# Fourth edge stage of a graph network: keys and values from 64-row matmuls on the two halves of the array

## The reference

```
q = (h @ Wq).reshape(n, 8, 16)                       # per node
wk = relu(edge_attr_64 @ k_w1 + k_b1) @ k_w2 + k_b2  # per edge, wv alike
k = sum_s sh[:, s] * (h[dst] @ Cqk[:, s, :]) * wk    # s = 0..8, 64 -> 128 columns
v = sum_s sh[:, s] * (h[dst] @ Cv[:, s, :]) * wv
attn = sum over 16 of q[src] * k                     # 8 heads
alpha = softmax of attn over the edges of a segment
x = x + batchnorm(h @ W_self + segment_sum(v * alpha) @ W_out)
```

## Time and profile before

| | |
|---|---|
| device time, three runs | 4099.88 us median, 4085.95 to 4110.83 |
| profiled execution, first to last instruction | 3379.4 us |
| fourth edge stage, first transposes to last product | 2145.3 to 3274.7 us |
| its steady part, 2260 to 3250 us | PE busy 982.8 of 990 us, DVE 864.9, POOL 700.0 |
| DMA in the steady part | 0.91 of 16 engines, 206 GB/s |
| granted TensorE clock there | 1.00 |

### The profile page before, as it was taken

One profiled execution on the slowest core, in us unless ns is written; L12 is line 12 of the kernel. 1 busy time (PEld: TensorE's weight loads), 2 busy tenths in 40 slices (PEclk: granted clock), 3 DMA queues, 4 the chain that ended last, 5 costly groups with the idle time before them and its releaser, 6 DMA issues. The chain is left out here.

```text
span 3379.4 us, 50406 instructions
## 1 busy us (share of the span) xinstructions
PE 2444.5 (72%) x13300; PEld 2060.6 (61%) x13300; DVE 2317.3 (69%) x5149; ACT 866.2 (26%) x2411; POOL 2061.6 (61%) x2125
## 2 busy tenths in 40 slices
PE   2887877614454444417777776599999999999986
PEld 2777776513343333315555554488888888888872
DVE  3555555417878888875555553378888888888885
ACT  1111111026455454401111111032222222222231
POOL 2777777147566665127777771577776767777620
PEclk7767677556555665759999996799999999999995
DMA  2444443155455554005555551898899989899940
GB/s 64 95 87 87 85 85 81 23 147 144 121 133 122 130 128 119 24 21 152 157 156 157 156 155 50 184 212 210 210 209 211 210 203 209 207 205 208 205 101 10
DMA packets 372188, 462.25 MB, mean 137 GB/s; under 512 B 199157, under 2 KB 236280, under 8 KB 372000
## 3 DMA queue, kind: packets, MB, share of 16 engines
q1 hardware_dynamic: 283808, 254.61, 33.7%
q0 software_dynamic: 73216, 150.93, 18.8%
q10 hardware_dynamic: 14976, 54.53, 4.7%
HBM read 394.55 MB, written 65.27 MB: 136 GB/s over the span
## 5 line engine op out<-in xcount | busy, mean ns | idle before, releaser
L1920 PE MATMUL psum<-ckv,z 128*128 128x256 f32 x4160 | 965.6, 382 | 0.0
L1920 PEld LDWEIGHTS psum<-ckv,z 128*128 128x128 f32 x4160 | 764.9, 191 | 97.1
L985 POOL DMA_INDIRECT ga<-T,src_i x416 | 428.6, 1030 | 306.3 <-PE psum L1098 115.7
L1813 POOL DMA_INDIRECT acc<-QW,dst_i x416 | 397.5, 956 | 186.2 <-issue 110.3
L1821 POOL DMA_INDIRECT ga<-XX,src_i x416 | 399.0, 959 | 170.2 <-issue 121.9
L275 POOL DMA_INDIRECT ga<-TA,src_i x416 | 410.6, 987 | 126.7 <-issue 126.7
L275 POOL DMA_INDIRECT ga<-T,src_i x416 | 394.3, 948 | 151.7 <-issue 124.3
L1967 DVE TENSOR_TENSOR z<-psum,shb 128x2560 f32<-128x2560 f32 x104 | 293.2, 2820 | 58.0 <-PE psum L1911 46.8
L455 PE MATMUL psum<-wre,re 128*128 128x68 f32 x832 | 216.8, 353 | 134.3 <-DVE oneT L331 74.3
L455 PEld LDWEIGHTS psum<-wre,re 128*128 128x128 f32 x832 | 175.9, 262 | 156.2 <-issue 151.9
L1628 DVE TENSOR_TENSOR acc<-acc,psum 64x128 f32 x416 | 118.6, 285 | 156.7 <-PE psum L1583 112.5
(11 more groups left out here) (346 smaller groups left out, 4315.7 us busy)
## 6 DMA issues: line engine op xcount, KB each, us to landing
shb<-in_ea SPq DMA_DIRECT2D x104, 640.0 KB
WKV<-wkvo ACTq DMA_DIRECT2D x104, 512.0 KB
shb<-in_ea SPq DMA_DIRECT2D x104, 512.0 KB
wkv<-WKV SPq DMA_DIRECT2D x104, 512.0 KB
dl<-DL SPq DMA_DIRECT2D x208, 128.0 KB, 3.3
win<-TB SPq DMA_DIRECT2D x416, 32.0 KB
ga<-T,src_i POOLq DMA_INDIRECT x832
ef<-in_ea SPq DMA_DIRECT2D x104, 128.0 KB
```

What stands on the lines that cost most here:

```text
L985: pool.indirect_dma_start(ga[:, ring(g) + t, :], None, T1, bass.IndirectOffsetOnAxis(ap=src_i[:, g * GT + t:g * GT + t + 1], axis=0)).then ...
L1813: pool.indirect_dma_start(qg[:, (g % QR) * GT + t, :], None, QW, bass.IndirectOffsetOnAxis(ap=dst_i[:, g * GT + t:g * GT + t + 1], axis=0) ...
L1920: last = pe.matmul(kv_of(k)[:, t, :], z[:, k % 2, j, t * 128:(t + 1) * 128], ckv[:, j, :], start=(j == 0), stop=(j == NZ - 1))
```

## The change

The nine sh slices are no longer paired on the two halves of the array. Instead the tiles are: tiles 0 and 1 of a group live on partitions 0 to 63, tiles 2 and 3 on 64 to 127, each with all NS = 9 slices of 64 rows. `z` and `shb` become [128, 9, 256]. XX has single-width rows (256 B), written once. The gathered tiles lie in the order 0, 2, 1, 3, so that two of them side by side are one 128-column transpose: two transposes a group. `products` runs, for t = 0, 1 and each slice, one 64-row matmul for tile t on the upper half and one for tile t + 2 on the lower half; the halves write different banks. `ckv` holds all nine slices on both halves. The zeroing of the padded slices goes. On the host `edge_attr_9` is laid out so that a half's 9 x 256 numbers are one run of 9216 B, read as two transfers a group. The step's loop over t has two turns instead of four, and the sums follow each turn.

```diff
                 sp.wait_ge(n3_dve, 8)
-                for a in range(2):
-                    sp.dma_start(XX.rearrange("(j p) f -> p j f", p=PN)[:, :, a * D:(a + 1) * D], H[:]).then_inc(n3_o, 16)
+                sp.dma_start(XX.rearrange("(j p) f -> p j f", p=PN), H[:]).then_inc(n3_o, 16)
...
-                        sp.dma_start(shb[0:D, k % 2], A["ea9"][0:NS:2, cols].partition_broadcast(D)).then_inc(e3_e[k % 2], 16)
-                        sp.dma_start(shb[D:128, k % 2, 0:NZ - 1], A["ea9"][1:NS:2, cols].partition_broadcast(D)).then_inc(e3_e[k % 2], 16)
+                        for half in range(2):
+                            sp.dma_start(shb[half * D:half * D + D, k % 2].rearrange("p s e -> p (s e)"),
+                                         A["ea9"][2 * g + half].partition_broadcast(D)).then_inc(e3_e[k % 2], 16)
...
-                    for t in range(GT):
-                        last = pe.transpose(bank[0][:, t * 128:(t + 1) * 128], ga[:, (k % GR) * GT + t, :], ident[:])
+                    for t in range(GT // 2):
+                        pair = (k % GR) * GT + 2 * t
+                        last = pe.transpose(bank[0][:, t * 128:(t + 1) * 128], ga[:, pair:pair + 2, :].rearrange("p a f -> p (a f)"),
+                                            ident[:])
...
-                    for j in range(NZ):
-                        last = pe.matmul(kv_of(k)[:, t, :], z[:, k % 2, j, t * 128:(t + 1) * 128], ckv[:, j, :],
-                                         start=(j == 0), stop=(j == NZ - 1))
-                    if t == GT - 1:
+                    for j in range(NS):
+                        for half in range(2):
+                            P = slice(half * D, half * D + D)
+                            last = pe.matmul(kv_of(k)[:, t + 2 * half, :], z[P, k % 2, j, t * 128:(t + 1) * 128], ckv[P, j, :],
+                                             start=(j == 0), stop=(j == NS - 1))
+                    if t == GT // 2 - 1:
...
-                    for t in range(GT):
+                    for t in range(GT // 2):
                         if kv:
                             products(*kv, t)
-                        if old and t == 0:
-                            sums(*old, 0)
-                        if old and t == 2:
-                            sums(*old, 1)
+                        if old:
+                            sums(*old, t)
+                        if p1 and t == 0:
+                            softmax_pe_1(pe, S3, q, 8)
                         if p1 and t == 1:
-                            softmax_pe_1(pe, S3, q, 8)
-                        if p1 and t == 3:
                             softmax_pe_2(pe, S3, q, 8)
...
-                    dve.tensor_tensor(z[:, k % 2], bank[0][:].unsqueeze(1).to_broadcast([128, NZ, GT * W]), shb[:, k % 2],
+                    dve.tensor_tensor(z[:, k % 2], bank[0][:, 0:PW].unsqueeze(1).to_broadcast([128, NS, PW]), shb[:, k % 2],
                                       ALU.mult).then_inc(e3_z, 1)
```

More of the change, by code:

```diff
@@ L1669, in build @@
         end_of_layer()
-        NZ = 5
+        PW = GT // 2 * W
         wq = sb("wq", [D, F])
-        ckv = sb("ckv", [128, NZ, 2 * F])
+        ckv = sb("ckv", [128, NS, 2 * F])
         w_out = sb("w_out", [F, D])
@@ L1679, in build @@
         sel_b = sb("sel_b", [24, 128])
-        XX = dram("XX", [N, 2 * D])
+        XX = dram("XX", [N, D])
         QW = dram("QW", [N, F])
@@ L1697, in _ @@
                 for m, w in ((ckv[:, :, 0:F], "Cqk"), (ckv[:, :, F:2 * F], "Cv")):
-                    L(m[0:D, :, :], A["L3_gnn_" + w][:, 0:NS:2, :])
-                    L(m[D:128, 0:NZ - 1, :], A["L3_gnn_" + w][:, 1:NS:2, :])
+                    for half in range(2):
+                        L(m[half * D:half * D + D, :, :], A["L3_gnn_" + w])
                 sp.wait_ge(n3_dve, 8)
-                for a in range(2):
-                    sp.dma_start(XX.rearrange("(j p) f -> p j f", p=PN)[:, :, a * D:(a + 1) * D], H[:]).then_inc(n3_o, 16)
+                sp.dma_start(XX.rearrange("(j p) f -> p j f", p=PN), H[:]).then_inc(n3_o, 16)
                 sp.wait_ge(n3_qc, len(rounds(NJ, 4)))
                 sp.dma_start(QW.rearrange("(j p) f -> p j f", p=PN), tab[:]).then_inc(n3_o, 16)
-                sp.wait_ge(n3_o, 3 * 16)
+                sp.wait_ge(n3_o, 2 * 16)
                 sp.wait_ge(n3_l, NL3 * 16)
@@ L1762, in build @@
         e3_n = [sem(f"e3_n{k}") for k in range(2)]
-        (e3_one, e3_oa, e3_X, e3_z, e3_wq, e3_V, e3_ev, e3_s, e3_S, e3_acc, e3_M, e3_Mx, e3_i, e3_pad) = [
+        (e3_one, e3_oa, e3_X, e3_z, e3_wq, e3_V, e3_ev, e3_s, e3_S, e3_acc, e3_M, e3_Mx, e3_i) = [
             sem("e3_" + x) for x in
-            ("one", "oa", "X", "z", "wq", "V", "ev", "s", "S", "acc", "M", "Mx", "i", "pad")]
+            ("one", "oa", "X", "z", "wq", "V", "ev", "s", "S", "acc", "M", "Mx", "i")]
         S3 = softmax_sems("b3", bank[7])
@@ L1770, in build @@
         SPARE = 8
-        ga = tmp("ga3", [128, GR * GT, F])
+        SLOT = (0, 2, 1, 3)
+        ga = tmp("ga3", [128, GR * GT, D])
         one = tmp("one3", [128, OR * GT, 128])
         wkv = tmp("wkv", [128, 2, GT, 2 * F])
-        shb = tmp("shb", [128, 2, NZ, GT * W])
-        z = tmp("z", [128, 2, NZ, GT * W])
+        shb = tmp("shb", [128, 2, NS, PW])
+        z = tmp("z", [128, 2, NS, PW])
         vw = tmp("vw", [128, UT, F])
@@ L1934, in body @@
                         softmax_pe_0(pe, S3, q, 8, am3[:, b])
-                    for t in range(GT):
+                    for t in range(GT // 2):
                         if kv:
                             products(*kv, t)
-                        if old and t == 0:
-                            sums(*old, 0)
-                        if old and t == 2:
-                            sums(*old, 1)
+                        if old:
+                            sums(*old, t)
+                        if p1 and t == 0:
+                            softmax_pe_1(pe, S3, q, 8)
                         if p1 and t == 1:
-                            softmax_pe_1(pe, S3, q, 8)
-                        if p1 and t == 3:
                             softmax_pe_2(pe, S3, q, 8)
+                        if p2 and t == 0:
+                            softmax_pe_3(pe, S3, q, 8)
                         if p2 and t == 1:
-                            softmax_pe_3(pe, S3, q, 8)
-                        if p2 and t == 3:
                             pe.wait_ge(S3["less"], q + 1)
@@ L1955, in _ @@
             def _(dve):
-                dve.memset(shb[D:128, :, NZ - 1, :], 0.0).then_inc(e3_pad, 1)
                 dve.memset(D3[:], 0.0).then_inc(e3_i, 1)
@@ L2168 @@
     a["ea64"] = np.pad(a.pop("edge_attr_64"), ((0, fill), (0, 0))).T
-    a["ea9"] = np.pad(a.pop("edge_attr_9"), ((0, fill), (0, 0))).T
+    ea9 = np.pad(a.pop("edge_attr_9"), ((0, fill), (0, 0)))
+    a["ea9"] = ea9.reshape(NT // GT * 2, GT // 2 * W, 9).transpose(0, 2, 1).reshape(NT // GT * 2, 9 * GT // 2 * W)
     a["L2_gnn_WT"] = a.pop("L2_gnn_W").T
```

9 lines of the change are left out of this document (2 added, 7 removed).

## The result

Before 4105.35 us (median of 4 runs, 4085.95 to 4114.69), after 4269.17 us (4 runs, 4250.63 to 4281.62); ratio 1.0402, 95% interval 1.0366 to 1.0437: 4% slower.

A forecast was written before the change was run, and what follows sets the result against it. PE was taken as the bound, hardly ahead of DVE. The stage's +7 us and -5 us ahead of it gave +2: span 3381 plus an unchanged 720.5, so 4102 us, range 4050 to 4500.

The forecast's parts named there:

- the first rival: Products on PE: halves overlap only across a pass's second half, 0.1635 us a pass, +387 us, 4482; chance 18%.
- The pace of the products, 0.111: Products on PE: 72 overlapping 64-row passes at 0.111 us each, 7.99 us a step, -0.65 a step.
- Rivals 1 and 2: Products on PE: partial overlap, 0.1635 us a pass, +387 us (18%); no overlap, 0.216 a pass, +780 us (13%).
- Change of mode, 0.12: PE switching between 128 and 64 rows: four changes a step at 0.12 us each, +0.48 us a step.
- z shorter: DVE's z: 2304 numbers a partition instead of 2560, 2.47 us start to start instead of 2.74, -0.27 a step.
- L628 waits 2.15 us a round: Sums now end PE's step, so PE waits 2.15 us for DVE at L628, once in four steps.
- Floor by POOL, transfers hidden: Fourth edge stage: POOL's pace, about 9.95 us a step, limits any gain to -88 us; no engine waits for DMA.
- The prologue's -5 us: Ahead of the stage: XX is written once, so the queries' write can start earlier, -5 us.
- I leave the 720.5 us to the median: Time around the profiled span: the 720.5 us up to the median stay as they are, added to span 3381.
- the gain on paper of 0.49 us a step: A plain step of PE: 9.91 us instead of 10.40, from transposes, products, sums and changes of mode.

The follow-up runs named there:

- before, again: The kernel before, no edit, profiled a second time: 4088.55 us against 4094.02, ratio 0.9974; span 4094.4 us.
- quick execution: The execution of the kernel before, no edit, caught by its first profile: span 3379.4 us; its own time is not on record.
- e3: The changed kernel with PE multiplying only five of the nine slices, 40 passes a step: 4113.44 us against 4094.02 of before (one run, about 1.005).
- e10: The changed kernel with only the upper half's products, tiles 2 and 3 left out, 36 passes a step: 4706.65 us against 4202.48 of before, ratio 1.1202.

## Why the prediction was right and wrong

4269 is inside the range of 4050 to 4500, but 167 us from the value of 4102, and beyond that value's own range of 4065 to 4165 (whose terms add up to 4176 at the upper end). That the range holds it is luck: it reached up to 4500 to take in the first rival, which did not happen. The direction is in part luck too: the value was 2 us above before, and most of the chance of slower came from the rivals. What happened was neither the forecast nor a rival: the forecast's mechanism held, and a term was missing.

- **The pace of the products, 0.111**: right. Pairs are 0.216 apart. Here trace and rule no longer differ: the loads' order of the earlier trace rows holds for equal rows only, and the rule of the Trainium skill (TensorE: Matmul & The Clock Gate, Part 3) that a load for the other row group is pulled ahead agrees with the 4.08 us for 36 passes. Rivals 1 and 2 would need 6 or 8 us for them. Their 31% was a misreading of rows that could not show the case.
- **Change of mode, 0.12**: about right: 4.08 - 18 x 0.216 = 0.19 for a change and the last pass's end; quiet steps of 10.01 us against 9.91 forecast.
- **z shorter**: 2553 ns against 2819, in proportion 2537. Right.
- **L628 waits 2.15 us a round**: right in place and cause, 2.90 us in the timeline above, but too cheap. By the waits it is 73.2 us in the stage, where 26 x 2.15 = 56 were forecast. But before, again already waits 45.1 us at L628, where the forecast had none, so the change added some 28. Moving both sums away takes 72 us off the time, about the 68 that the wait loses. The clock fell in the pause (0.80 us for two products), yet the stage's mean is the same without it, 0.828 against 0.825.
- **Floor by POOL, transfers hidden**: the floor was never reached, POOL waits 663 us for DVE; and loads of one slice of nine change nothing. The prologue's -5 us can't be told in spans that differ by 150.
- **"I leave the 720.5 us to the median"**: this step failed. I took the gap between span 3379.4 and time 4100 for something ahead of and behind the program. It was inside: the second profile has late instructions and a mean clock of 0.744 over its span, the first had neither in this stage. So the sum ran on a PE that was always supplied and always at its upper clock.
- **The missing term**: 72 passes a step instead of 40, put at nothing beyond their pace. In the quick execution 40 passes cost only that; 72 were never seen in one. In the ordinary ones after has 205 us more of lateness in the stage. Columns split in before shows the price alone: +128 us, 3.1%. As an estimate, that with the sums' place at 1.5%, less the gain on paper of 0.49 us a step (51 us, 1.2%), makes 3.4% against the 4.0 measured; the parts come from other kernels and other chips, and need not add.

What stays open: what makes an instruction late. The places in the loop point to how the list of instructions is supplied. Against it, the packets that bring PE's list, 48 of 16 KB in this stage in both profiles of before, take as long in the quick execution (median 1.20 us) as in the other (1.18), and e3 has many late instructions with few passes. No run separated fetching from recording or anything else. Nor is it known why the first profile had none, or what after would take in such an execution.

## What to carry to other kernels

When the time and the profiled span differ by hundreds of microseconds, as here, take a second profile of the same kernel before any working: the first was of an execution unlike the ones timed, and the sum on it was 167 us off. On a PE-bound loop count instructions as well as columns: twice as many passes at equal work cost 3.1% here, half as many gave 1.3%; why is not known. Wherever a sum or a reduction that another engine waits for is moved to the end of a step, ask what is left to cover it; one wait of 2 to 3 us here also took the clock away for the products behind.

## What the hardware showed beside

- With the products of 64 rows on one half of the array alone the clock did not come up (e10): PE busy for 684.65 of 700 us, granted 0.50, in the whole stage. With both halves in turn the quiet window has 1.00. I had thought of the clock as a matter of PE being busy.
- A semaphore can be raised long after the matmul that raises it has ended: in before, again, that of L654 came 8.3 us late, and ACT's L671 with it.
- The same kernel's spans: 3379.4 and 4094.4 us. The stage alone took 1129 and 1530.
